# All tables of turns of a two-stream decoder kernel placed anew, with 671 idle products in a pass instead of 117

## The reference, cut to what matters

```
x = x + _L0_attn_ref(_layernorm(x, axis=-1), ...)    # delta rule with convolutions and a router
x = x + _L0_xattn_ref(_layernorm(x, axis=-1), ...)   # cross attention, 16 heads
x = x + _L0_ffn_ref(_layernorm(x, axis=-1), ...)     # gated feed-forward
...                                                  # L1: causal attention, mixer, 8 experts
...                                                  # L2: attention with rope, cross attention, 14 experts
...                                                  # L3: state-space scan, cross attention
x = x + _L3_ffn_ref(_layernorm(x, axis=-1), ...)     # 8 experts with a capacity over all tokens
```

## Time and profile before

| | us |
|---|---|
| median of 3 runs | 4543.98 |
| lowest and highest of them | 4533.97 to 4562.33 |
| span of the profiled execution | 4543.7 |
| first stretch (from 10.2 us on) | 205.1 |
| seven rounds | 542.5 to 546.8 each |
| last stretch | 430.3 |
| final stage | 81.9 |

### The profile page before, as it was taken

One profiled execution on the slowest core, in us unless ns is written; L12 is line 12 of the kernel. 1 busy time (PEld: TensorE's weight loads), 2 busy tenths in 40 slices (PEclk: granted clock), 3 DMA queues, 4 the chain that ended last, 5 costly groups with the idle time before them and its releaser, 6 DMA issues. The chain is left out here.

```text
span 4543.7 us, 93495 instructions
## 1 busy us (share of the span) xinstructions
PE 3844.6 (85%) x37090; PEld 2702.1 (59%) x37090; DVE 3103.1 (68%) x8220; ACT 2006.0 (44%) x4862; POOL 650.2 (14%) x988
## 2 busy tenths in 40 slices
PE   3788898888878888788898889888898888889886
PEld 3565565656656665565665656655565655666664
DVE  4467767576775768667686776767767676775782
ACT  2244463443535345363443535345463443535441
POOL 2010201101020110101101011110201101021003
PEclk7788988898988989788897988989988887988997
DMA  6000000000000000000000000000000000000002
GB/s 156 1 2 1 9 1 9 2 1 9 1 9 1 8 2 1 9 1 8 2 7 3 1 8 2 9 2 1 9 1 9 2 1 9 1 8 2 1 1 96
DMA packets 52803, 45.61 MB, mean 10 GB/s; under 512 B 8354, under 2 KB 48914, under 8 KB 52126
## 3 DMA queue, kind: packets, MB, share of 16 engines
q1 hardware_dynamic: 48076, 33.04, 2.7%
q0 software_dynamic: 2560, 5.79, 0.3%
q10 hardware_dynamic: 1714, 0.54, 0.1%
HBM read 27.25 MB, written 12.62 MB: 9 GB/s over the span
## 5 line engine op out<-in xcount | busy, mean ns | idle before, releaser
L763 PE MATMUL banks<-scratch 32*128 32x512 f32 x2048 | 497.0, 708 | 28.6 <-DVE scratch L909 10.8
L331 ACT ACT_TABLE_LOAD x299 | 383.6, 1283 | 7.5 <-PE banks L1090 2.2
L873 ACT ACTIVATE scratch<-banks 128x512 f32<-128x512 f32 x512 | 277.2, 599 | 199.9 <-PE banks L797 199.0
L909 DVE TENSOR_REDUCE scratch<-banks 128x4 f32<-128x512 f32 x512 | 321.8, 680 | 39.1 <-PE banks L736 16.5
L1601 PE MATMUL banks<-scratch,w_ident 128*128 128x256 f32 x1024 | 289.1, 407 | 53.4 <-DVE scratch L1752 52.6
L1885 PE MATMUL banks<-scratch 32*32 32x32 f32 x10496 | 270.4, 217 | 68.2 <-issue 52.8
L1746 DVE TENSOR_TENSOR_SCAN scratch<-scratch 128x512 f32<-128x512 f32 x256 | 312.8, 1222 | 11.5 <-ACT scratch L1689 6.2
L1885 PEld LDWEIGHTS banks<-scratch 32*32 32x32 f32 x10496 | 236.6, 130 | 117.3 <-issue 73.9
L1689 ACT ACTIVATE scratch<-scratch,ssm_A 128x256 f32<-128x256 f32 x512 | 228.6, 505 | 112.0 <-DVE scratch L1746 102.9
L763 PEld LDWEIGHTS banks<-scratch 32*128 32x128 f32 x2048 | 167.8, 203 | 185.1 <-DVE scratch L909 56.3
L1227 PE MATMUL banks<-experts,scratch 128*128 128x128 f32 x1792 | 243.6, 281 | 9.4 <-ACT scratch L1263 8.4
(11 more groups left out here) (522 smaller groups left out, 8414.1 us busy)
## 6 DMA issues: line engine op xcount, KB each, us to landing
expert_in<-scratch SPq DMA_DIRECT2D x1, 4112.0 KB, 28.8
experts<-in_e_W SPq DMA_DIRECT2D x14, 256.0 KB, 5.5
scratch<-expert_in SPq DMA_DIRECT2D x2, 1542.0 KB, 10.8
w_e_W<-in_e_W SPq DMA_DIRECT2D x3, 704.0 KB
experts<-in_e_w SPq DMA_DIRECT2D x1, 1792.0 KB, 9.8
experts<-in_e_w SPq DMA_DIRECT2D x2, 896.0 KB, 13.5
scratch<-expert_in SPq DMA_DIRECT2D x2, 514.0 KB, 5.2
0_xres<-in_x SPq DMA_DIRECT2D x8, 128.0 KB, 2.1
```

The source lines that it names most:

```text
L331: act.preload_act_table_set(name)
L763: last = pe.matmul(row_tiles(t), lhs[r, col(s)], rhs[r, s], start=True, stop=letter == "S" and mask is None, skip_group_check=True)
L873: P.give(act.activation(pT[:, s % 2, j, :], t, ACT.Exp), f"{nm}.T{s}{j}")
L909: P.give(dve.tensor_reduce(negm[:, s, NI * j:NI * j + NI], row_tiles(t), X, ALU.max, negate=True), f"{nm}.S{s}{j}")
```

## The change

All ten strings are replaced; the code that reads them is the same, and so are the first stretch and the final stage. Every engine still gets the same steps of each stream, in the same order inside a stream. What differs is how the steps of the streams alternate, and where and how many idle products stand on TensorE. The diff, cut to the beginning of the strings:

```
 TURNS = [
-    ("111ww0001000011010111000111100101wwwwww101111110011000100000001100000000011011011111101111010011011100000000"
-     "1110www00011111111010111111111111111111111111111111101001111101101111101111100110110001111110100000110111110"
...
+    ("w10w1wwwwwwww00www10000w1w0wwwwwwww1wwwwwwwwwwwwwwwwwwwwwwwwwwwwwwwwwww0ww0wwwwwwwwwwwwwwwwwwwwwwwwww10w0ww"
+     "wwwww1wwwwwwwwwwww1www101w0w11www0w1www1w1ww1wwww10w11111w11w0www01www1010w000w0w0w1wwwwwww1ww001wwwww0w01w"
...
-    ("111000111000000000101111100111100000000011000000111101111001011001100000000000111111111011111111111011101111"
...
+    ("01010101000000001101011110111110000100011001010011100101001001010101010000010100011111011111110101111101111"
...
-    ("110010111111000111001100111101100000000110000000000001100110000001000001100111111111110111100000011111010011"
...
+    ("01010101000100111011011101001110111010000000001100000010001110001010100111101010011111001110001010101010110"
...
-    ("110010000000001110000001110000000110111101101111001111011100011111110000101110"),
+    ("010101000000100111000000110000001101101111001111010111011101101011110000111100"),
     ("111000"),
 ]
 LAST_TURNS = [
...
-     "1000www0000wwwwwwwww01111101011111110011001000000000000011100w000010"),
...
+     "wwwwwwwwwwwwwwwwwwwwwwwwwwwwwwwwwwwwwwwwwwwwwwwwwwwwwwwww"),
...
-    ("11001"),
+    ("110010"),
 ]
```

More of the change, by code:

```diff
@@ L86 @@
-    ("110010000000001110000001110000000110111101101111001111011100011111110000101110"),
+    ("w10w1wwwwwwww00www10000w1w0wwwwwwww1wwwwwwwwwwwwwwwwwwwwwwwwwwwwwwwwwww0ww0wwwwwwwwwwwwwwwwwwwwwwwwww10w0ww"
+     "wwwww1wwwwwwwwwwww1www101w0w11www0w1www1w1ww1wwww10w11111w11w0www01www1010w000w0w0w1wwwwwww1ww001wwwww0w01w"
+     "w00ww0w00ww1www00ww1111000011110110101011111000100101010111101w010001011w11w1w11w1w1w1111111111110111001011"
+     "101110101111111111011011111111100www1w1111110w01011010111ww001ww01000w10www101wwwwww0ww11w01w1www100ww0w0w1"
+     "wwww11w11ww01w1ww1wwwww11www10w0111wwww00001www11101w11011011w1w00w1wwww111ww0wwww1wwww1w1w0wwwwww0w11ww101"
+     "0110001101w011011111010011110000101001w0wwwww0ww1w01w0ww1w10w0w00w101w0wwww0ww11w10w00000001001110w00111ww1"
+     "0010110w1wwww00ww00010w1000ww01wwwww00w00ww000w0www00www00000www00w000010w0w00wwwwww0w0101111wwww00w0wwwwww"
+     "ww100www0wwwwww1ww0100www0w000w1w01011000000w10ww0w0www0wwwwwwwwwwwwwwwwwwwwwwwwwwwwwwwww0wwwww0wwwwwwww100"
+     "wwwww1w1ww1w0w0www01110110100000000000001w0011011w11101101101001000100001ww1001100000011011011101000w001111"
+     "0011000000000000000000w00w1010100001111000001w01wwww10wwww000001w0www0www1www010w00w0101wwwwwwwwwww11ww011w"
+     "www1w10wwwwwwww10w0www1wwwwwwwww1w0w0w1w1w0w1w1ww000w1wwwwww000ww1www1w01wwwwwww0w0w0w0w0ww1001w0w010w00www"
+     "wwww11w00ww0ww00ww0w0w01wwwwwwwwww00w0www0w0www1w0w01ww011w0w00ww0w0wwwww000wwww1wwww0w0w00wwwwww0ww0ww0w1w"
+     "w0www1www0wwwwww0wwww00w01110111w01w010111010w111w0w1w0011w01w00w1wwwwww1w000w10w00w1w0ww1www0w1w1ww1ww0www"
+     "wwww10ww1wwww01wwwwww1w01ww1111101101111101ww1w11111w1w1111111111111111111111111111111"),
@@ new lines @@
+    ("01010101000000001101011110111110000100011001010011100101001001010101010000010100011111011111110101111101111"
+     "01001011111100111110111011111100111110111001101111101110011001011100110000011010001011000011001010000100110"
+     "00010011101010011000000011111001001101100001010000100000111010101010000000111110111000011010001101100010101"
+     "01001100000101111000000001010010000110001001110101100001000000001000110011011001110100010011110100101001100"
+     "101101111101101100000110111101110111111111"),
@@ new lines @@
+    ("01010101000100111011011101001110111010000000001100000010001110001010100111101010011111001110001010101010110"
+     "00001011100100100001111001001110110001010001011101100111111101101101110101111000110011011101101001000101000"
+     "01011011111011110111110100101011001101111000011100011110110001010001000000000010010000111000000010010000011"
+     "00011101111011101100101111001010110000001001010110111000011011110011010001111100110111110010011101111001000"
+     "01100111101111111100000100100000100010101100000000110100000011001000010101100000110110011101100100001000100"
+     "00000111110000111010011001011011101111111111111111111"),
@@ L97 @@
[L97 to L105, removed]
@@ L106 @@
-    ("110001000000001100010000000000011100000000111100001010"),
-    ("11001"),
+    ("10ww1wwwwwww0ww1w0w100w001www01wwwwwwww0www1ww0wwwwwww0wwww0wwwwww1wwwwwwwwwwwwwwwww0w1w01www010w1w1ww1w1w1"
+     "wwwwww1w11www0w10ww1110ww101www1w00w1w0w0w001w0ww1w0w000000000001001000000000010w0ww000ww0011w1w1w1111w1w11"
+     "0wwww001w1w1w01www1w0010w1ww1wwwwwww1w0w0wwww10w11w01w11ww110101w001101000011100011100010011110001111101101"
+     "100100110111101110101010110010101000000000000001001110111001101001w000w0w0wwww1wwwwwwwwww01ww00000000011000"
+     "0000000101www00010001110010010000010000000010000001100001wwwwwwwwwwww0wwwwww0wwwwww0wwwwwwwww0wwww000wwwwww"
+     "www0110011100100010000000100010w11110110w1w10w0ww0w1www0ww01w100000000000000w000www1w110110w100w0ww010w1011"
+     "w01100100111100000000110110100010010001100000100000000100000000000000000011w01110ww000110w01ww1wwwww10ww10w"
+     "0ww100ww0w01www0wwwwwwww011ww0w0wwwwwwww0ww0wwwww0w1w0wwwwwwww1wwwwwwwwwwwwwwww0ww00wwww0wwwww00www00wwwwww"
+     "w0w0www01wwww0w0wwwww0ww00w1ww0w0w0w1wwww0ww1wwwwwwww0w10w1w0w0ww0ww0www0wwwww1ww0ww0www00ww0ww0www000ww0ww"
+     "1www1wwww0www00w00ww0w1w10w110wwww0ww1ww001wwwwww1w0wwww00www1wwww00ww0w00wwwwwww0wwwwwww11w0wwwwwwwww0w1ww"
+     "ww1ww0wwwwwww0w0ww0www000w0w01w0w0w000ww0ww0www0wwwwwww0000wwwwwwwwwwwwwwwwww0wwww0wwwwwwwwwwwww0wwwwwwwwww"
+     "wwwwwwwwwwwwwwwwwwwwwwwwwwwwwwwwwwwwwwwwwwwwwwwwwwwwwwwww"),
@@ new lines @@
+    ("10101000100110000001011110110111000100100101000000000100000000000000011111001101010101000001001111111100100"
+     "01101010001101111111110000101111110001111001110000010000011010110010100010011001101101111101010011000100101"
+     "01000001000001100100100000010000000100000000110000000001001000000000000000000000000001010000000010100000000"
+     "00100000000101010011010100100100000000"),
+    ("01101011111110010001010100100111110000001000000000001101001101000000100011000111011100000111100010000110000"
+     "01000101100100000000010100101001000011010000101000010000000001000000101000101101000100100000101000011001000"
+     "10010000000010000100000000000101111010010100101110000110000000001110000001011011101111011010101010110011010"
+     "00000000111000111100001110110110000000000001001011100100001100000000011000000001001100000000110100010000000"
+     "0001000000000"),
@@ L108 @@
+    ("101010000000010100000110000000010100000000111110000100"),
+    ("110010"),
 ]
```

## The result

The changed kernel takes 4293.1 us, median of four runs (4290.1 to 4297.0); before it was 4543.7, and the ratio is 0.9456 with a 95% interval of 0.9428 to 0.9484. That is 250 us, 5.4%, faster. I had forecast 4421 us, 2.7%: the right side, at half the size. The profiled execution took 4291.5 us, with a span of 4289.5.

The account below looks back on a forecast made before the run. TensorE was taken as the nearest bound, with waits across engines and half-clock time. Seven rounds at -17 us (-21 + 7 - 3) give -119, last stretch -2, final stage -2: 4544 to 4421 us; range 4270 to 4610, likeliest case 4300 to 4498.

Parts of the forecast that it names:

- What bounds the kernel: In the round: TensorE nearest, no engine alone; the rest is steps waiting across engines, with 131 us at half clock.
- Part 3, the alternation: In the rounds: fewer table loads, -3 us each; the rest of the new order 0, ten us either way.
- Rival D: Whole kernel: the order itself is won or lost, clock unchanged; counted within A and B, no chance of its own.
- A: Rounds and last stretch: idle products stand in the way, +16 us a round, 4670 us; chance 0.22.
- B: Whole kernel: nothing gained, as VectorE and ScalarE chains and overshoot eat the clock's gain, say 4540 us; chance 0.18.
- Part 1, the clock: In the rounds: idle products win back 70% of 47 us of TensorE's time, shortening a round by 21 us.
- The experts' product: Sign at L1219 in the changed profile: its mean duration would come nearer to 382 ns, its full-clock time.
- Part 2, the products' own time: In the rounds: 554 more products lie mostly inside waits; overshoot costs 7 us a round; L3_mamba's misfit by 6 us.
- the ramp rule: Whole kernel: ramp penalty under 1% of a span, so under 45 us to win and a time within 1% of before.
- weight-load busy time: In the round: as TensorE's metric it leaves 216 us of room, products costing near 0, some 50 us lower time.
- Part 4 and the last stretch: At the kernel's end: -2 us for the final stage's start, and -2 us in all for the last stretch.
- C: Whole kernel: nearly all the clock gain, clock 0.98 or more, 40 us of a round, 4239 us; chance 0.13.

Follow-up runs that it names:

- new_none: The new order of turns with no idle product, against the kernel before: 4365 us, ratio 0.9619.
- after: The changed kernel itself, new order with 671 idle products in a round and 613 in the last stretch: 4293 us, ratio 0.9456 to the kernel before.
- after_twice: The changed kernel with every idle product made twice, 1342 in a round and 1226 in the last stretch: 4717 us, ratio 1.0399 to the kernel before.
- old_none: The old order of turns with no idle product at all, against the kernel before: 4562 us, ratio 1.0045.
- old_many: The old order with the new tables' 671 (last stretch 613) idle products ahead of the same steps, against the kernel before: 4760 us, ratio 1.0476.
- after_loads2: The changed kernel with every activation table load requested twice, though the second load was never made: 4298 us, ratio 0.9461 to the kernel before.

## Why the prediction was right and wrong

**What bounds the kernel**: right as far as it went. No engine alone set the time, and the waits between the engines did. But I read the half-clock time as something that only products could remove; in new_none the order alone took the round's clock from 0.84 to 0.90.

**Part 3, the alternation**: the step that failed. I wrote "By whole sections the streams stand as before, so I price it at 0, with ten us of a round either way in the range". Without products it is 548 to 520 us a round (means of the seven), 28 us, nearly three times the edge that I gave it; in all some 195 us. That the streams stand alike by whole sections was no reason for a price of 0: between the same places the 806 turns of TensorE's string can alternate in many ways. Rival D, "the order itself is what is won or lost", was left "within A and B by size" and had no chance of its own; it was the case. The table loads, taken at -3 us a round, stay unpriced between 0 and 9 us; I had also counted 8 fewer in a round by the strings, where the traces show 7.

**Part 1, the clock**: the mean clock of the round was forecast at "0.95 or so" and is 0.96. As a number the 70% came true (0.88 to 0.96 is two thirds of what was missing), but the order has a share in it, which the forecast gave to the products. L0_delta's 0.91 is a little short of the "above 0.92", and L2_moe is 0.91 instead of 0.82, with only its 7 products. The experts' product stayed at 427 and 411 ns (418 and 422 before) and didn't come nearer to 382. How the time follows was forecast too high: in new_none to after, the mean clock goes from 0.884 to 0.950 and the time by 72 us, for everything the products do.

**Part 2, the products' own time**: the net of -21 + 7 a round, -98 us in seven rounds, measured some 53 us for the whole kernel (1.18 points, after's 1.63 less the 0.45 of before). How the shortfall divides between clock and overshoot stays open: leaving out the short runs gave some 27 us, but that is their cost less what their clock was worth. That 187 products don't fit into L3_mamba by 6 us was right for the old order, and too low (13.9 us longer), and wrong for the new one, which has 14.4 us idle there instead of 10.4.

**The two rules that the prediction named**: by the ramp rule of the Trainium skill, page "TensorE: Matmul & The Clock Gate", Part 1, under 1% of a typical span is lost to the ramp. Clock and products together gave 1.6% in the new order; the rule is nearer than my 21 us a round, though a quarter of a round was at half clock. By the Trainium skill, page "Trainium Kernel Development and Optimization", Performance Expectations, weight-load busy time is the good metric and matmul busy time a bad one; I had worked out from it that the products would cost near 0. after_twice doesn't bear that out: at 66% weight loads in after, 73% of the further products' time is paid.

**Part 4 and the last stretch**: -2 each was forecast; the last stretch gave 14.9, of which the order is 4.9 (437.5 us in old_none, 432.6 in new_none), and the final stage half a microsecond.

**Rivals**: A's mechanism, products that cost more than they bring, has been seen in old_many (+4.8% on before) and after_twice (+4.0%), but not in the change. The forecast case was 4300 to 4498 us, and the 4293 lie just below it. C, with a chance of 0.13 for anything below 4300, forecast a place near the result, 4239 us, for the wrong reason, a clock worth 40 us a round. The direction was luck in good part: the mechanism that I forecast gave 1.2 of the 5.4 points, and the term that I had put at 0 gave the rest.

## What to carry to other kernels

When two streams share in-order engines, don't price a new one at zero because the streams stand alike by whole sections; run it once without anything else that came with it. Counts of alternations didn't tell the fast orders from the slow ones here. Idle products are worth having only in waits of the order in which they stand, and it is worth trying them without the shortest runs; here runs of one and two cost more than they brought, and a set of products moved to another order cost 4%. A low clock may be the shadow of waits: the order with fewer waits had 0.884 instead of 0.845 with no idle product. And look in the trace whether an added instruction is there before reading a price from its run.

## What the runs showed of the hardware that was not expected

- TensorE's granted clock and the time can part company: 0.896 at 4760 us, 0.884 at 4365 us, 0.960 at 4717 us, 0.932 and 0.950 at the same 4291 to 4293 us.
- With idle products of 128 columns instead of 256 the clock over the whole kernel was 0.932 instead of 0.950, and 0.921 instead of 0.944 without the short runs.
- A second request for the same activation table right behind the first leaves no load in the trace of after_loads2 (277 loads in all with it and without it), while 28 loads that the kernel doesn't ask for stand there, 22 of them at the experts' activation L1273.
